# First expert layer of a four-layer decoder: rows of tokens fetched into expert slots by indirect transfers, return matrices compared with the slots' tokens on two engines

## The reference

```python
idx, w = _router(x, gate_w, e_bias)                  # 6 of 64 experts a token, and their gates
pos = (cumsum(one_hot) - one_hot) ...                # the token's place among its expert's tokens
keep = pos < 64
xd = zeros((64, 65, 256)).at[e_flat, slot].set(x[tok])   # the tokens, sorted into the slots
h  = relu(einsum('ecd,eid->eci', xd, w1)) ** 2       # 64 experts, 256 -> 128
yd = einsum('eci,edi->ecd', h, w2)                   # 128 -> 256
y  = zeros((T, D)).at[tok].add(yd[e_flat, slot] * gate * keep)
```

## Time and profile before

| | us |
|---|---|
| median of 3 runs (2243.59 to 2246.06) | 2245.22 |
| the profiled execution | 2248.22 |
| its span | 2246.4 |
| mean granted clock of TensorE | 0.977 |
| first expert layer, first routing step to its last combination | about 133 to 375 |
| PE busy, of the span | 95% |
| DVE, POOL, ACT busy, of the span | 66%, 63%, 44% |

### The profile page before, as it was taken

How to read it: one execution, slowest core, us unless ns; L and a number is a source line. 1 busy time by engine, 2 the same in 40 slices (tenths; PEclk the granted TensorE clock), 3 DMA queues, 4 the chain that set the end, 5 groups by cost and what they waited for, 6 DMA issues and landing times.

```text
span 2246.4 us, 36279 instructions
## 1 busy us (share of the span) xinstructions
PE 2135.7 (95%) x13980; PEld 1489.9 (66%) x13984; DVE 1477.2 (66%) x2546; ACT 993.2 (44%) x1530; POOL 1406.8 (63%) x876
## 2 busy tenths in 40 slices
PE   7898999899999998998999999999997999999998
PEld 5686877656566565665566565588895566565588
DVE  6776753577777757666787777653334777777653
ACT  4452333445454445211554544444434554554443
POOL 0356663288888874463888888634441888888634
PEclk9899999999999998998999999999998999999999
DMA  3126864332223104002223222025523223222012
GB/s 94 42 87 197 263 229 143 74 76 62 56 63 76 42 29 133 25 1 60 56 56 83 56 56 70 18 88 153 148 64 73 56 61 78 56 56 70 16 55 79
DMA packets 65708, 179.65 MB, mean 80 GB/s; under 512 B 11280, under 2 KB 21280, under 8 KB 65154
## 3 DMA queue, kind: packets, MB, share of 16 engines
q1 hardware_dynamic: 65154, 177.01, 29.4%
q10 hardware_dynamic: 384, 0.33, 0.1%
HBM read 162.32 MB, written 14.98 MB: 79 GB/s over the span
## 4 chain that ended last, share of the span: by engine, by line
PE 80%; DVE 7%; POOL 3%; issue 3%; DMA 2%; ACT 2%; SPq 1%; POOLq 0%; DVEq 0%; ACTq 0%
PE psum L1468 20%; PE psum L1478 20%; PE psum L930 18%; PE psum L1396 8%; PE psum L1495 2%; PE psum L1400 2%; PE psum L1636 2%; PE psum L1593 1%; PE psum L944 1%; PE psum L1323 1%; DMA kt_scratch<-kt 1%; POOL CL L1942 1%; PE psum L1201 1%; DMA bd<-in_blockdiag 1%; DVE mx L2449 1%
## 5 line engine op out<-in xcount | busy, mean ns | idle before, releaser
L1920 ACT ACTIVATE E<-psum 125x896 f32<-125x896 f32 x576 | 520.2, 920 | 577.1 <-PE psum L1468 554.5
L2465 DVE TENSOR_REDUCE mx<-psum 128x1 f32<-128x500 f32 x945 | 561.9, 668 | 127.6 <-PE psum L1400 70.6
L2203 POOL TENSOR_TENSOR SA<-SA,E 125x896 f32<-125x896 f32 x282 | 595.1, 2110 | 69.5 <-ACT E L1920 50.9
L1478 PE MATMUL psum<-E,V 125*64 125x448 f32 x2304 | 472.2, 545 | 0.0
L1396 PE MATMUL psum<-KH,QH 64*128 64x500 f32 x864 | 331.5, 402 | 19.7 <-DVE mx L2449 17.9
L1478 PEld LDWEIGHTS psum<-E,V 125*64 125x64 f32 x2304 | 162.9, 136 | 233.4 <-issue 176.9
L1468 PE MATMUL psum<-QH,KH 64*125 64x448 f32 x1152 | 282.4, 414 | 2.4 <-ACT E L1920 2.4
L2203 POOL TENSOR_TENSOR SA<-SA,SB 125x896 f32<-125x896 f32 x93 | 194.2, 2089 | 124.8 <-DVE SB L2483 77.3
L1468 PE MATMUL psum<-QL,KH 64*125 64x448 f32 x1152 | 271.2, 364 | 0.0
L1468 PE MATMUL psum<-M,ones 64*125 64x448 f32 x1152 | 270.8, 363 | 0.0
L1468 PE MATMUL psum<-QH,KL 64*125 64x448 f32 x1152 | 242.9, 363 | 0.0
(11 more groups left out here) (305 smaller groups left out, 3996.8 us busy)
## 6 DMA issues: line engine op xcount, KB each, us to landing
KH<-kt_scratch SPq DMA_DIRECT2D x96, 375.0 KB, 5.2
KL<-kt_scratch SPq DMA_DIRECT2D x96, 375.0 KB, 7.0
EW<-in_f_w SPq DMA_DIRECT2D x64, 256.0 KB, 8.3
kt_scratch<-kt SPq DMA_DIRECT2D x16, 750.0 KB, 8.1
WS<-in_f_w SPq DMA_DIRECT2D x31, 384.0 KB, 4.4
GB<-gates_scratch SPq DMA_DIRECT2D x36, 224.0 KB, 3.9
slot_of_t<-slots_scratch SPq DMA_DIRECT2D x64, 112.0 KB, 4.4
WoT<-in_a_WoT SPq DMA_DIRECT2D x24, 256.0 KB, 3.7
```

The lines of the kernel that those rows point to most:

```text
L1478: i = e.matmul(psum[c * DC:(c + 1) * DC, 4, 0:HT], V[0:LP, b, k * DC:(k + 1) * DC], E[g[n, b, k] % NE][0:LP, half[c]], start=k == 0, stop= ...
L1920: e.activation(E[m % NE][0:LP, :].rearrange("p (c q) -> p c q", c=2), psum[0:LP, pair:pair + 2, 0:HT], ACT.Exp).then_inc(exp_set.sem, 1)
L2203: e.tensor_tensor(SA[b % 2][0:LP, :], a[0:LP, :], x[0:LP, :], ALU.add).then_inc(sum_set.sem, 1)
L2465: e.tensor_reduce(mx[:, b % 2, j * 3 + c:j * 3 + c + 1], psum[:, bank, 0:CW], AX.X, ALU.max).then_inc(small_free.sem, 1)
```

## The change

Tokens are no longer summed into the slots by matmuls. A 17th column of W4 holds the token's number plus 1, so that `gsl` gives, beside the gates, the number of the token in each slot (0 in an empty one). After `gturn` DVE makes from it the row to fetch, the number, and its negative. POOL then issues one indirect transfer for each pair (`gather`), which fetches 128 rows of 1 KB from a DRAM copy of the tokens (YS) to the 128 slots; 8 transposes on PE replace the 28 matmuls of a group's two `disp` (and the 14 products that filled the wait before the first). S is now made by comparing 1..896, loaded once, with the slot's token number: even pairs on POOL, odd ones on ACT in two activations (|t - n|, then max(0, 1 - that)). The scratch of slot numbers, its transposes and its 64 broadcast loads go, and so do YtH and YtL. The order of the list is new: `gsl` of the next group comes first in a group, its `gturn` and gathers third, its `disp` tenth and thirteenth; six context steps stand before group 0, and two places of each group take none. S has four buffers.

```diff
     c["slots"] = np.concatenate([slot, token], 1).astype(f)     # token = i * 128 + p + 1
+    c["tokens"] = np.tile((np.arange(T) + 1).astype(f), (P, 1))
 (sparse_order)
-    order += [("route", 6)] + [("st", 0, a) for a in range(4)] + [("route", 7), ("disp", 0, 0), ("swrite",), ("tables",), ("route", 8), ("disp", 0, 1)]
-    order += [("st", 1, a) for a in range(4)] + [("pload", q) for q in range(3)] + [("wload", e) for e in range(8, 12)]
+    gather = lambda g: [("gather", 4 * g + x) for x in range(4)]
+    order += [("route", 7), ("route", 6)] + [("st", 0, a) for a in range(4)] + [("tables",), ("gsl", 0), ("st", 1, 0), ("gturn", 0)] + gather(0)
+    order += [("pick", 0)] + side.pop(0) + side.pop(0) + [("st", 1, 1)] + side.pop(0) + side.pop(0) + [("st", 1, 2)] + side.pop(0) + [("st", 1, 3)]
+    order += [("disp", 0, 0)] + side.pop(0) + [("disp", 0, 1)] + [("wload", e) for e in range(8, 12)]
-        steps = [([("gsl", 0)] if g == 0 else []) + [("ups", g)] + (pick(0) if g == 0 else []), pick(q) if g > 0 else [("gturn", 0)],
-                 [("comb", q - 1)] if g > 0 else [], ([("disp", g + 1, 0)] if more else []) + st(0) + (pick(1) if g == 0 else []),
-                 [("downs", q), ("downs", q + 1)], (pick(q + 1) if g > 0 else []) + st(1), [("comb", q)],
-                 ([("disp", g + 1, 1)] if more else []) + st(2), [("downs", q + 2), ("downs", q + 3)],
-                 pick(q + 2), [("comb", q + 1)] + st(3),
-                 [("gsl", g + 1)] if more else [], pick(q + 3), [("comb", q + 2)] + ([("gturn", g + 1)] if more else [])]
+        steps = [([("gsl", g + 1)] if more else []) + [("ups", g)], ([("comb", q - 1)] if g > 0 else []) + [("pick", q + 1)],
+                 ([("gturn", g + 1)] + gather(g + 1) if more else []) + st(0), [("downs", q), ("downs", q + 1), ("pick", q + 2)], [],
+                 [("comb", q)] + st(1), [("downs", q + 2), ("downs", q + 3), ("pick", q + 3)], [],
+                 [("comb", q + 1)] + st(2), ([("disp", g + 1, 0), ("pick", q + 4)] if more else []), [], [("comb", q + 2)] + st(3),
+                 [("disp", g + 1, 1)] if more else [], []]
-            if side:
+            if side and n not in PAUSES:                        # PAUSES = (4, 13)
 (pe_experts, disp)
-                    for k, y in enumerate((m["YtH"], m["YtL"])):
-                        p = e.matmul(psum[:, bank, :], y[:, i, kd * P:(kd + 1) * P], m["ST"][g % 2][:, i, :], ...)
+                for x in range(4):
+                    if kd == 0:
+                        e.wait_ge(*gathered.at(4 * g + x))
+                    p = e.transpose(psum[:, bank, x * P:(x + 1) * P], m["XG"][(4 * g + x) % 8][:, kd * P:(kd + 1) * P], ident[:, :])
 (act_experts)
+            elif kind == "pick" and t[0] % 2 == 1:
+                e.wait_ge(*gs_set.at(g))
+                e.activation(m["away"][:, :], m["tokens"][:, :], ACT.Abs, bias=m["ntok"][g % 2][:, x:x + 1]).then_inc(*act_own.up())
+                e.wait_ge(*act_own.now())
+                if q >= 4:
+                    e.wait_ge(*combined.at(q - 4, 1))
+                e.activation(m["S"][q % 4][:, :], m["away"][:, :], ACT.Relu, bias=ones[:, 0:1], scale=-1.0).then_inc(s_act.sem, 1)
 (pool_experts)
+            elif kind == "gather":
+                e.wait_ge(*gs_set.at(g))
+                if g >= 2:
+                    e.wait_ge(*picked_in.at(g - 2, 1))
+                e.indirect_dma_start(m["XG"][q % 8][:, :], None, YS[:, :],
+                                     bass.IndirectOffsetOnAxis(m["row"][g % 2][:, x:x + 1], 0)).then_inc(gathered.sem(q), 16)
 (dve_experts, gturn)
+                if g >= 2:
+                    e.wait_ge(*s_act.at(4 * g - 5))
+                    e.wait_ge(*s_pool.at(4 * g - 6))
+                    e.wait_ge(*picked_in.at(g - 2, 1))
+                token = psum[:, upper_bank[f, (kind, g)], 0:68].rearrange("p (q r) -> p q r", r=17)[:, :, 16]
+                e.tensor_scalar(m["row"][g % 2][:, :], token, -1.0, 0.0, ALU.add, ALU.max)
+                e.tensor_scalar(m["ntok"][g % 2][:, :], token, -1.0, None, ALU.mult)
+                e.tensor_copy(m["tok"][g % 2][:, :], token)
 (sp_experts, route 0)
+                e.dma_start(YS.rearrange("(i p) d -> p i d", p=P), Y[:, :, :]).then_inc(ys_out.sem(), 16)
+                e.dma_start(m["tokens"][:, :], io["tokens"]).then_inc(tokens_in.sem(), 16)
```

More of the change, by code:

```diff
@@ L8 @@
 F32, F32R, BF16 = mybir.dt.float32, mybir.dt.float32r, mybir.dt.bfloat16
+U32 = mybir.dt.uint32
 ALU = mybir.AluOpType
@@ L608, in build @@
     at(norm_at)
-    m["YtL"] = mem.take("YtL", [P, NT, D], F32R)
+    m["away"] = mem.take("away", [P, T], F32)
+    m["S"] = [mem.take("S", [P, T], F32R)]
+    assert mem.at <= norm_end
     at(folded_at)
-    m["YtH"] = mem.take("YtH", [P, NT, D], F32R)
+    m["XG"] = [mem.take("XG", [P, D], F32) for _ in range(8)]
     m["pos"] = mem.take("slot_of", [P, NT, E0], F32)
-    m["W4"] = mem.take("w_pairs", [P, NT, E0 // 2, 4], F32R)
+    m["W4"] = mem.take("w_pairs", [P, NT, NG, 17], F32R)
     assert mem.at <= base
@@ L617, in build @@
     emask = mem.take("expert_mask", [P, NT, E0], F32)
-    m["PB"] = [mem.take("slot_of_t", [P, T], BF16) for _ in range(2)]
-    m["gs"] = [mem.take("slot_gate", [P, 4], F32) for _ in range(2)]
-    m["S"] = [mem.take("S", [P, T], F32R) for _ in range(2)]
+    m["tokens"] = mem.take("tokens", [P, T], F32)
+    for name, d in (("gs", F32), ("tok", F32), ("ntok", F32), ("row", U32)):
+        m[name] = [mem.take(name, [P, 4], d) for _ in range(2)]
+    m["S"] += [mem.take("S", [P, T], F32R) for _ in range(2)]
     st_at = mem.at
@@ L810, in build @@
     r_set = flag("r_set", ups)
-    prod_set = flag("prod_set", [u for u in ups if SWIGLU[u[0]]])
+    prod_set = flag("", [u for u in ups if SWIGLU[u[0]]], st_set)
     gated = flag("gated", [u for u in per_ffn("gate") if u[1] >= FFN_FREE[u[0]]])
@@ L817, in build @@
     ot_turned, x_back = flag("ot_turned", back_groups), flag("x_back", back_groups)
[L820 to L823 removed]
+    groups = [(g,) for g in range(NG)]
     picked_in, xd_set = flag("picked_in", done(FFN[0], "disp")), flag("xd_set", done(FFN[0], "disp"))
@@ L875, in build @@
     eb_in, tri_in, rope_k_in = one("", after=v0_in), one("", after=wq_out), one("", 2, after=fold0_a)
-    ss_out = one("", after=tri_in)
+    ys_out, tokens_in = one("", after=tri_in), one("tokens")
     ln_in = one("", after=eb_in)
@@ L882, in build @@
     wraw_in = Landed(nc, "wraw", 3, [(k, (k,)) for k in range(3)])
-    pb_in = Landed(nc, "", 3, [(q % 3, (q,)) for q in range(E0 // 2)], 2, after=wraw_in)
-    wq_in = Landed(nc, "", 3, [(k, (k,)) for k in range(3)], after=pb_in)
+    gathered = Landed(nc, "gathered", 4, [(q % 4, (q,)) for q in range(E0 // 2)])
+    wq_in = Landed(nc, "", 3, [(k, (k,)) for k in range(3)], after=wraw_in)
     heads_in = Landed(nc, "heads", 4, [(g, (g,)) for g in range(4)], 2)
@@ L1982, in act_project_turn @@
         act_turn(e, TURNED_NORM[n], i, 4 + i % 4)
-        if n == 0:
-            e.activation(ffn[0]["YtH"][:, i, :], Y[:, i, :], ACT.Copy).then_inc(tokens_high.sem, 1)
     def act_square(e, i):
@@ L2241, in pool_experts @@
         m = ffn[f]
-        for i in tiles if f == 0 else ():
-            e.wait_ge(*tokens_high.at(i))
-            e.tensor_tensor(m["YtL"][:, i, :], Y[:, i, :], m["YtH"][:, i, :].bitcast(F32), ALU.subtract).then_inc(tokens_low.sem, 1)
         for kind, *t in FFN[f]:
```

118 lines of the change are left out of this document (52 added, 66 removed).

## The result

| | before | after |
|---|---|---|
| median of 4 runs each | 2244.4 (2239.2 to 2246.1) | 2301.8 (2298.6 to 2308.7) |
| span of the profiled execution | 2246.4 | 2306.9 |
| `ups` of group 0, of group 1 | 171.0, 202.2 | 192.3, 227.1 |
| start of `ups`, group 6, group 7 | 323.3, 345.3 | 383.4, 404.0 |
| end of the layer (first transpose of the sum, OT) | 375.5 | 432.6 |

The kernel is slower: ratio 1.0259, 95% interval 1.0242 to 1.0275. The forecast was 2232.3. The profiled execution of the kernel after is the slowest of its four (2308.7). Of its 60.5 us more of span 57.1 lie in the layer, and 3.4 behind it. So single runs are compared by the end of the layer, not by their total.

What follows compares the result with a forecast made beforehand. PE was taken to set the pace at 24.2 us a group; -19.1 + 5.3 - 2.7 + 3.6 = -12.9 us took 2245.2 to 2232.3. The range was 2213 to 2258.

Steps and rivals of the forecast that it cites:

- `ups` of group 1: Start of the layer: group 1 starts at 207.5 instead of 202.2, +5.3 us.
- groups 1 to 5: Middle of the layer: five groups take 102.0 us instead of 121.1, -19.1.
- group 6: Next-to-last full group: 19.3 us instead of 22.0, -2.7.
- group 7: Last group with the tail: a new wait for the next layer's weights, +3.6 us.
- behind the layer: Rest of the kernel: no change; over a microsecond of change in its length would make the forecast wrong.
- the three rivals: Gathers hidden, 2218.9 us (chance 0.20); DVE becomes the bound, 2244.2 (0.18); gathers dear and kernel slower, 2261.0 (0.20).
- the pitch: Time per group in groups 1 to 5: PE's 18.5 us plus 1.9 of waiting for gathers, 20.4.
- The second rival: DVE becomes the bound in groups 1 to 5: its own waits stay, pitch 22.9 us, total 2244.2; chance 0.18.
- The gather: POOL's indirect transfers, four a group: 1.1 us an issue and 3.0 us to land.
- The path: From gturn to the first disp: DVE's numbers 1.0, four issues 4.4, landing 3.0, together 8.4 us.
- The third rival: Gathers are dear: PE waits 6.0 us at each group's first disp, pitch 24.5, total 2261.0; chance 0.20.
- The start: Chain of gates, gathers and rotations ahead of group 0: its ups starts at about 187.0, 16 us later.

Runs made afterwards that it cites:

- e1: The changed kernel with the context rotation's sine products made on DVE instead of POOL; 2263.3 us, end of the layer 392.4.
- j1: Changed kernel with sine products on POOL one batch ahead, ups before gsl, comb one pair later, gsl(g+2) ending group g, context steps at all places; 2264.3 us.
- i1: e1 with ups ahead of gsl, and gsl, gturn and gathers of group g+2 at the end of group g; 2273.0 us.
- h1: e1 with ups ahead of the next group's gsl, and every comb one pair later; 2277.5 us.
- e3: The changed kernel with the dispatch by 28 matmuls a group again, no gathers, the tokens' low half left out; 2278.0 us.

## Why the prediction was wrong

By its own terms, in the profiled execution:

| step | forecast | measured | with the hold gone (e1) |
|---|---|---|---|
| `ups` of group 1 | +5.3 | +24.9 | +7.8 |
| groups 1 to 5 | -19.1 | +35.1 | +12.7 |
| group 6 | -2.7 | -1.4 | -2.1 |
| group 7 | +3.6 | -1.6 | -1.6 |
| behind the layer | 0 | +3.4 | -1.9 |

The last line is within the noise: what lies behind the layer spans 11.3 us in the runs, so the prediction's sign of a change of more than a microsecond there could not tell anything.

**The step that failed** is the sentence "Behind a gather that waits for DVE's numbers stand `crot` and the next comparison; both have over a microsecond of room there." It counted POOL's free time (15 of 20.4 us busy) where the order of its queue decided. The rotation had no room: DVE waits for it, and PE for DVE. DVE stood 8.31 us in the instance above (group 0) and 27.2 in groups 1 to 5, and taking the hold away gives 21.9 to 30.7 of the 35.9 us back that the layer takes more from its first `ups` on. None of the three rivals named it.

**The second failed step** is the pitch: 18.5 us of PE's content plus one wait of 1.9. With the hold gone (e1) it is 26.8: PE is busy for 21.2 of it, at a clock of 0.85 instead of 0.99, and stands for 5.6. The prediction put the slower clock at nothing in groups 1 to 5, and of PE's waits it counted the gathers and 0.3 us of YDL. PE's own work did shrink (97.0 us busy in groups 1 to 5 of j1 at clock 0.90, 116.6 before), but two ways showed: downs to comb (14.3 us of waiting in e1, 18.3 in i1, 4.5 before) and `gsl` to the gathered rows (21.4 in h1). That the 28 products had been their cover is argued and not shown: for the first way e3 speaks for the order of the list (14.0 us with the products, at new places), and h1's later comb took that wait away. The second rival had the right reason, "If they stay, since they come from the order of the list", but took DVE's waits as a constant 5.7 a group; its 22.9 was reached by no kernel, with 24.7 (j1) as the best.

**The gather.** Forecast 1.1 an issue; measured 0.95 busy and 0.30 between, 1.25 apart, and the first of four 1.90 where it meets an ST part. Landing forecast 3.0, measured 5.9 in the median, from the issue on. The path, 8.4, was 10.7 in h1, and 1.6 of the 2.3 us more are the issues. The third rival put the break-even at 1.55 us an issue, and the distance stayed below it; its place, PE's wait at the first `disp`, holds only 1.4 us in the kernel after. Its sign was right for another reason, which is luck.

**The start.** Forecast 187.0 for the first `ups`, measured 192.3. DVE's gates take 6.4 us, not 3.9:

```profile
154.70 1.58 DVE L2650 TENSOR_TENSOR w<-scores,expert_mask 128x448 f32<-128x448 f32 x1
...
158.26 1.29 DVE L2658 TENSOR_TENSOR w<-w,wsum 128x448 f32<-128x448 f32 x1
...
161.11 0.61 DVE L2646 SCALAR_TENSOR_TENSOR slot_of<-expert_mask,psum 128x448 f32<-128x448 f32 x1
```

The first was 0.61 in the earlier trace rows; moved ahead, it runs beside POOL's products of the shared expert (154.39 to 155.80, 156.81 to 159.07). The rotations alternate between POOL and DVE as forecast, but two of POOL's products take 1.85 us and not 0.98; each starts beside an ST part of DVE (181.03 to 182.25, 185.96 to 187.18):

```profile
181.25 1.85 POOL L2281 TENSOR_TENSOR ctx_rot<-V,sin_k 125x384 f32<-125x384 f32 x1 [2.20 <-DVE V L2779]
183.06 0.99 POOL L2282 TENSOR_TENSOR ctx_rot<-V,sin_k 125x384 f32<-125x384 f32 x1
186.18 1.85 POOL L2281 TENSOR_TENSOR ctx_rot<-V,sin_k 125x384 f32<-125x384 f32 x1 [2.13 <-DVE V L2779]
```

In group 0 (34.8, forecast 20.5) lie a slow clock, 0.63, behind PE's idle time ahead of it (`ups` alone 6.96 instead of 3.68, where 1.7 us was added for a slow start), and then the first hold.

**Groups 6 and 7.** Group 6 went as forecast in direction, by half (-1.4). The new wait of 3.6 us in group 7 did not come: the last kt was issued at 399.01 and the load behind it at 402.31, so the store held it for 3.3 us and not for the 7.1 of the earlier trace rows. PE's first product with these weights started at 407.67 without a wait, 11.7 us behind the last `cturn` (forecast 10.8). Why that store was quick is open.

**Chances.** 0.21 stood on slower, and the range ended at 2258; the sum of the rivals had no case in which a queue's order, rather than a price, decides.

## What to carry to other kernels

An instruction that waits for another engine's late result is as long, for all behind it in its queue, as its wait: when one is put on an in-order queue, list what stands behind it and who waits for that, and do not compare busy times. Work that is taken from the bounding engine may also have been cover for the others' round trips, and a new order of the list has a price of its own (e3). Before such work is counted as gain, add up each closed way (here `gsl`, turn, numbers, four issues, landing, and downs, YDH, YDL, comb): here each was the next wait when another had gone. And compare single runs by the end of the changed stage: outside it these differed by up to 11 us with nothing changed.
